# Context rows of a gated cross-attention kernel added by GpSimd besides vector, with the plan's places set anew

## What is computed

```python
txt_proj = jnp.einsum('btd,de->bte', textual_features, Ws)
feat_proj = jnp.einsum('bfd,de->bfe', features, W)
h = jnp.tanh(txt_proj[:, None, :, :] + feat_proj[:, :, None, :] + b[None, None, :, :][..., 0, :])
rho = jnp.einsum('bftd,d->bft', h, w[:, 0])
...
att = jax.nn.softmax(rho, axis=-1)
txt_h = jnp.einsum('bft,btd->bfd', att, textual_features)
w_s = jnp.tanh(jnp.einsum('bfd,od->bfo', txt_h, Wcw) + bcw)
b_s = jnp.tanh(jnp.einsum('bfd,od->bfo', txt_h, Wcb) + bcb)
return w_s * features + b_s
```

## Time and profile before

| | us |
|---|---|
| median of 3 runs | 1027.43 |
| lowest, highest | 1023.06, 1028.69 |
| span of the profiled execution | 1025.4 |
| TensorE products busy | 934.7 |
| ScalarE busy | 674.1 |
| GpSimd busy | 219.0 |

### The profile page before, as it was taken

The page is one execution under the profiler, slowest core; times in us unless marked ns, Lnnn a source line. Parts: engine busy times, 40 slices in busy tenths (PEclk is TensorE's granted clock), DMA queues, the critical chain, the costliest instruction groups (busy, mean ns, idle before and its releaser), DMA issues. The chain is left out here.

```text
span 1025.4 us, 22330 instructions
## 1 busy us (share of the span) xinstructions
PE 934.7 (91%) x8078; PEld 742.7 (72%) x8078; DVE 748.9 (73%) x1959; ACT 674.1 (66%) x983; POOL 219.0 (21%) x250
## 2 busy tenths in 40 slices
PE   8689999989988799999999999999999999985773
PEld 5557887779988787777777878888888887842331
DVE  3787988862222389978869869868876997795995
ACT  2122222201100069999999999989997998899992
POOL 1014543540112222312212211202211211220000
PEclk9579999999998899999999999999999999989886
DMA  7826677948996866756756667768777776410000
GB/s 247 338 62 236 244 267 283 351 174 279 331 338 227 272 232 226 236 165 219 237 175 228 211 202 253 267 219 277 266 253 231 268 260 220 149 32 12 2 22 21
DMA packets 137456, 218.68 MB, mean 213 GB/s; under 512 B 14113, under 2 KB 79138, under 8 KB 137346
## 3 DMA queue, kind: packets, MB, share of 16 engines
q1 hardware_dynamic: 119202, 156.55, 45.9%
q10 hardware_dynamic: 8592, 34.60, 8.7%
q0 software_dynamic: 9552, 26.10, 7.2%
HBM read 159.14 MB, written 58.06 MB: 212 GB/s over the span
## 5 line engine op out<-in xcount | busy, mean ns | idle before, releaser
L1287 PE MATMUL bank<-rowsT,expert_w 128*128 128x128 f32 x2656 | 328.3, 278 | 0.5 <-DVE rowsT L1053 0.5
L1287 PEld LDWEIGHTS bank<-rowsT,expert_w 128*128 128x128 f32 x2656 | 319.1, 194 | 9.5 <-issue 5.1
L748 ACT ACTIVATE tanhs<-shared_w,txtT 128x512 f32<-128x512 f32 x276 | 174.3, 718 | 24.5 <-issue 18.4
L748 ACT ACTIVATE arena<-shared_w,txtT 128x512 f32<-128x512 f32 x272 | 172.1, 720 | 0.0
L1458 PE MATMUL bank<-expert_w,act 128*128 128x256 f32 x664 | 162.4, 388 | 0.0
L1458 PEld LDWEIGHTS bank<-expert_w,act 128*128 128x128 f32 x664 | 121.7, 193 | 30.6 <-issue 17.3
L728 ACT ACTIVATE act<-bank 128x512 f32<-128x512 f32 x83 | 48.9, 589 | 114.2 <-PE bank L1287 114.2
L643 POOL DMA_DIRECT2D rows_by_expert<-rows_out x71 | 42.0, 592 | 371.4 <-DVE rows_out L1082 349.2
L654 POOL DMA_INDIRECT picked<-rows_by_expert,slot_of x64 | 75.9, 1186 | 157.6 <-issue 93.9
L1484 PE MATMUL bank<-arena,pick_w 128*32 128x256 f32 x1200 | 79.2, 389 | 3.2 <-ACT arena L737 2.3
L1484 PE MATMUL bank<-tanhs,pick_w 128*32 128x256 f32 x1112 | 74.4, 412 | 7.3 <-ACT tanhs L737 4.7
(11 more groups left out here) (257 smaller groups left out, 1392.1 us busy)
## 6 DMA issues: line engine op xcount, KB each, us to landing
expert_w<-in_WgT SPq DMA_DIRECT2D x71, 512.0 KB, 3.9
expert_w<-in_WuT SPq DMA_DIRECT2D x71, 512.0 KB, 5.2
expert_w<-in_WdT SPq DMA_DIRECT2D x71, 512.0 KB, 6.9
rows_by_expert<-tanhs ACTq DMA_DIRECT2D x8, 4096.0 KB, 14.3
rows_in<-rows_by_expert SPq DMA_DIRECT2D x71, 128.0 KB, 6.1
rows_by_expert<-rows_out POOLq DMA_DIRECT2D x71, 128.0 KB, 5.6
expert_w<-in_WgsT SPq DMA_DIRECT2D x12, 512.0 KB, 3.8
expert_w<-in_WusT SPq DMA_DIRECT2D x12, 512.0 KB, 4.6
```

The costliest lines, as they stand in the source:

```text
L748: got = e.activation(tiles[ec][:, S * j:S * (j + 1)], featT[ec], ACT.Tanh, bias=txtT[:, ec, t + j:t + j + 1])
L1287: got = e.matmul(bank[:, i * P:(i + 1) * P], w[:, at:at + P], t[:, c * P:(c + 1) * P], start=c == 0, stop=c == DC - 1)
```

## The change

Some pairs that were direct are now added by GpSimd: POOLS gives their number in each batch, counted over the pairs that vector does not add, and at most as many as there are of those. Its numbers sum to 77; in batch 7 there are 15 such pairs for 19, so 73 pairs result. A step `pooladd` does on GpSimd what `preadd` does on vector: two tensor_scalar of 128x512 for a channel half, after waiting for the feature copy and for the sum of the pair 8 before. ScalarE then waits for it and takes the pair in one activation. The next batch's feature copy on vector waits for the last of these adds, besides the last direct pair. PAIRS goes from 79 to 64 pairs, JOINS from 111 to 115. PLACES and LAGS get new numbers, which also puts the shared weights' load ahead of batch 0's x. The change is also described as letting tanh read the features in PSUM; there is no line for that in the diff, and featT stays in SBUF. The added pairs of batch 6 and 7 afterwards (v by vector, P by GpSimd, . direct, pair 0 first) are:

```diff
@@ -33,33 +33,39 @@
 
 ENGINES = ("sync", "gpsimd", "scalar", "vector", "tensor")
 
-PLACES = {"shared": -2.5, "zeroed": 62.5, "gap": 0, "opened": 25.5, "att_norm": 120, "att_norm_long": 30.5, "attend": 90,
-          "attend_long": 23.5, "moe_norm": 62, "moe_norm_long": 28, "route": 28, "route_long": 34, "late": -59, "gather": 4.5,
-          "norm": 2, "add": 7, "mix_in_end": -0.5, "join": 6.5, "sum": 5, "preadd": 4, "mix_out": 9.5, "mix_out_end": 49}
-
-
-PAIRS = {0: 18, 1: 9, 2: 12, 3: 0, 4: 0, 5: 0, 6: 13, 7: 27}
-JOINS = {0: 16, 1: 8, 2: 6, 3: 28, 4: 24, 5: 28, 6: 1, 7: 0}
+PLACES = {"shared": -2.5, "zeroed": 54, "gap": 0, "opened": 38, "att_norm": 120, "att_norm_long": 29.5, "attend": 90,
+          "attend_long": 23, "moe_norm": 62, "moe_norm_long": 28, "route": 28, "route_long": 33.5, "late": -58, "gather": 4.5,
+          "norm": 2, "add": 7, "mix_in_end": -0.5, "join": 7, "sum": 5, "preadd": 4, "pooladd": 4.5, "mix_out": 9.5,
+          "mix_out_end": 49}
+
+
+PAIRS = {0: 17, 1: 12, 2: 6, 3: 0, 4: 0, 5: 0, 6: 12, 7: 17}
+POOLS = {0: 5, 1: 10, 2: 5, 3: 8, 4: 1, 5: 16, 6: 13, 7: 19}
+JOINS = {0: 16, 1: 9, 2: 6, 3: 28, 4: 28, 5: 28, 6: 0, 7: 0}
 
 
 WARM = {"start": 14, "turn_rho": 2, "turn_q": 4, "linear": 0}
 
 
 LAGS = {
...
-    "gpsimd": {"narrow": 1.5, ("power", "att"): -3.5, ("power", "lin"): -2, "scatter": -0.5},
...
+    "sync": {"fetch": -17.5, "keep": 7.5, "linear": 1.5, "load_late": -2.5, "load_shared": -11.5, "load_side": -6, "load_x": 1.5,
+               "narrow": 0.5},
+    "gpsimd": {"gather": -1, "narrow": 0.5, "pooladd": -1.5, ("power", "att"): -3.5, ("power", "lin"): -2, ("power", "mix"): -2,
+               ("power", "moe"): 1, "scatter": -1},
...
@@ -177,6 +183,12 @@
 
         pairs, share = self.T // 2, int(PAIRS[b])
         return m * share // pairs != (m + 1) * share // pairs
+
+    def pooled(self, b, m):
+
+        rest = [k for k in range(self.T // 2) if not self.added(b, k)]
+        pairs, share = len(rest), min(int(POOLS[b]), len(rest))
+        return m in rest and rest.index(m) * share // pairs != (rest.index(m) + 1) * share // pairs
 
     def joined(self, b, m):
 
@@ -236,6 +248,10 @@
                     for ec in range(2):
                         early = max(at, at + 2 * m + ec - PLACES["preadd"])
                         place([[("preadd", b, ec, m)]], early, early)
+                if self.pooled(b, m):
+                    for ec in range(2):
+                        early = max(at, at + 2 * m + ec - PLACES["pooladd"])
+                        place([[("pooladd", b, ec, m)]], early, early)
                 if self.joined(b, m):
                     late = at + 2 * m + PLACES["join"]
                     place([[("join", b, m)]], late, late)
@@ -443,6 +459,7 @@
         s_shared_mm, s_x_shared = sem("shared_product"), sem("x_shared_added")
         s_added = sem("x_expert_added")
         s_wide_in, s_wide, s_sum = sem("wide_added"), sem("wide_tanh"), sem("rho_product")
+        s_pool_in = sem("wide_added_by_pool")
         s_joined, s_larger, s_swapped = sem("wide_joined"), sem("larger_ready"), sem("features_swapped")
         s_rho, s_rho_sub, s_rho_e = sem("rho_read"), sem("rho_less_max"), sem("rho_exp")
         s_ws, s_squash, s_affine, s_applied = sem("weighed"), sem("squashed"), sem("affine_ready"), sem("x_affine")
@@ -641,6 +658,17 @@
                     tile = e.value_load(tile_at[0:1, r:r + 1], min_val=0, max_val=ABSENT + 7)
                     e.wait_ge(s_row_bank, row_no["narrow", n] + 1)
                     e.dma_start(rows_dram[bass.ds(tile * P, P), :], rows_out[r % OUTS][:, :]).then_inc(s_stored[r % OUTS], 16)
+                elif name == "pooladd":
+                    b, ec, m = k
+                    q = pair_of(b, m)
+                    w = halves_of[q % PAIR][ec]
+                    bank, use, _ = misc["feature", b, ec]
+                    e.wait_ge(s_misc[bank], use)
+                    if q >= PAIR:
+                        e.wait_ge(s_sum, q - PAIR + 1)
+                    t = b * T + 2 * m
+                    e.tensor_scalar(w[:, 0:S], featT[ec], txtT[:, ec, t:t + 1], None, ALU.add)
+                    e.tensor_scalar(w[:, S:2 * S], featT[ec], txtT[:, ec, t + 1:t + 2], None, ALU.add).then_inc(s_pool_in, 1)
                 elif name == "gather":
                     b, j = k
                     u = 2 * ST * b + j
@@ -735,6 +763,9 @@
                     if plan.added(b, m):
                         e.wait_ge(s_wide_in, wide_in_no[b, DC - 1, m] + 1)
                         e.activation(wide_pair[q % PAIR], wide_pair[q % PAIR], ACT.Tanh).then_inc(s_wide, 1)
+                    elif plan.pooled(b, m):
+                        e.wait_ge(s_pool_in, pool_in_no[b, DC - 1, m] + 1)
+                        e.activation(wide_pair[q % PAIR], wide_pair[q % PAIR], ACT.Tanh).then_inc(s_wide, 1)
                     else:
                         if m == 0:
                             for ec in range(DC):
@@ -760,6 +791,8 @@
                     e.activation(weighed[:, 0, :], weighed[:, 0, :], ACT.Tanh, bias=scal[:, BCW:BCW + 1])
                     e.activation(weighed[:, 1, :], weighed[:, 1, :], ACT.Tanh, bias=scal[:, BCB:BCB + 1]).then_inc(s_squash, 1)
 
+        pool_in_no = {s[1:]: i for i, s in enumerate(s for s in plan.of["gpsimd"] if s[0] == "pooladd")}
+        assert list(pool_in_no) == sorted(pool_in_no, key=lambda k: (k[0], k[2], k[1]))
         wide_in_no = {s[1:]: i for i, s in enumerate(s for s in plan.of["vector"] if s[0] == "preadd")}
         joined_no = {s[1:]: i for i, s in enumerate(s for s in plan.of["vector"] if s[0] == "join")}
         assert list(wide_in_no) == sorted(wide_in_no, key=lambda k: (k[0], k[2], k[1])) and list(joined_no) == sorted(joined_no)
@@ -1106,7 +1139,10 @@
                 elif name == "feature":
                     b, ec = k
                     bank, done = product(("feature", b, ec))
-                    read = [m for m in range(T // 2) if b and not plan.added(b - 1, m)]
+                    read = [m for m in range(T // 2) if b and not plan.added(b - 1, m) and not plan.pooled(b - 1, m)]
+                    pool = [k for k in pool_in_no if k[0] < b]
+                    if pool:
+                        e.wait_ge(s_pool_in, pool_in_no[pool[-1]] + 1)
                     if read:
                         e.wait_ge(s_wide, pair_of(b - 1, read[-1]) + 1)
                     if wide_in_no and b and plan.added(b - 1, T // 2 - 1):
```

More of the change, by code:

```diff
@@ L45 @@
+PAIRS = {0: 17, 1: 12, 2: 6, 3: 0, 4: 0, 5: 0, 6: 12, 7: 17}
+POOLS = {0: 5, 1: 10, 2: 5, 3: 8, 4: 1, 5: 16, 6: 13, 7: 19}
+JOINS = {0: 16, 1: 9, 2: 6, 3: 28, 4: 28, 5: 28, 6: 0, 7: 0}
 WARM = {"start": 14, "turn_rho": 2, "turn_q": 4, "linear": 0}
 LAGS = {
-    "sync": {"fetch": -21, "load_side": -5.5, "narrow": 0.5},
-    "gpsimd": {"narrow": 1.5, ("power", "att"): -3.5, ("power", "lin"): -2, "scatter": -0.5},
-    "scalar": {"gate_act": 1, "soft_rho": -0.5, "softmax": -1, "spread": -2, "squash": 2, "tanh": 1, ("turn", "att"): -0.5,
-               "turn_e": -3.5, "zero": 8},
@@ L53 @@
-    "vector": {"add": 1.5, "add_bias": 4, "affine": 0.5, ("aggr", "att"): 1, ("aggr", "lin"): -0.5, ("aggr", "mix"): 1.5,
-               ("aggr", "moe"): -0.5, "apply": 2.5, "choice": -1, "convert": -16.5, "gate_act": 2.5, "join": -1, "larger": -9,
-               "linear": 3.5, "narrow": 1.5, ("newton", "att"): -2, ("newton", "lin"): -1.5, ("newton", "mix"): 0.5,
-               ("newton", "moe"): 1, "opened": 1.5, "pads": -1, "place": -0.5, ("power", "att"): -0.5, ("power", "lin"): 1,
-               ("power", "mix"): 0.5, ("power", "moe"): -1.5, "rho": -4, "side": -7, "sigmoid": -0.5, "soft_rho": -1, "softmax": 0.5,
-               ("stats", "att"): 2.5, ("stats", "mix"): 3.5, "step": -0.5, "stretch": 1, "sums": 1.5, "swap": -4, "text": -0.5,
-               "tiles": 2, ("turn", "mix"): -0.5, ("turn", "moe"): -4, "turn_q": 0.5, "turn_rho": -1, "turn_rows": 1, "weigh": -1,
-               "weigh_ws": -0.5},
@@ L61 @@
-    "tensor": {"count": 2, "feature": -0.5, "larger": -2, "logits": -2.5, "narrow": 0.5, "scores": -1.5, "spread": 3, "sum": -1,
-               "text": -1, ("turn", "att"): -1, "turn_e": -3.5, "turn_rho": -3, "up": -1, "weigh": -0.5},
+    "sync": {"fetch": -17.5, "keep": 7.5, "linear": 1.5, "load_late": -2.5, "load_shared": -11.5, "load_side": -6, "load_x": 1.5,
+               "narrow": 0.5},
+    "gpsimd": {"gather": -1, "narrow": 0.5, "pooladd": -1.5, ("power", "att"): -3.5, ("power", "lin"): -2, ("power", "mix"): -2,
+               ("power", "moe"): 1, "scatter": -1},
@@ new lines @@
+    "scalar": {"gate_act": 1, "soft_rho": -0.5, "softmax": -1.5, "spread": 3.5, "squash": 2, "tanh": 1, ("turn", "att"): -0.5,
+               ("turn", "moe"): -2, "turn_e": -2, "zero": -3.5},
+    "vector": {"add": 1, "add_bias": 4, "affine": -1, ("aggr", "att"): 0.5, ("aggr", "lin"): 0.5, ("aggr", "mix"): 1,
```

(11 more changed lines are left out.)

## The result

The changed kernel takes 1174.89 us (median of 4 runs, 1173.96 to 1177.77), the one before 1027.6 (median of 4; the table ahead has 3 of them): a ratio of 1.147 (95% interval 1.144 to 1.151), 147 us slower. The forecast was 1019 us with a range that ended at 1038. The profiled execution has a span of 1173.2.

What follows compares the result with a forecast made beforehand. Two bounds in series: TensorE to about 900 us, then ScalarE. From 1027.4 us, 8.4 off for ScalarE, 1.9 off for joins, 2 added for the feature chain: 1019 us; own range 1013 to 1024, 8-in-10 range 1011 to 1038.

Steps and rivals of the forecast that it cites:

- GpSimd's adds: the unknown cost: Price of one 128x512 add on GpSimd: taken as 0.8 us, bounds 0.47 to 0.86, so 3.2 us a pair.
- Costed at nothing, on that cover: GpSimd's adds stand 7 plan steps ahead of their tanh, 10 us in batch 5, 6.3 in batch 7: cost 0.
- GpSimd paces batch 7: Rival: adds of 0.86 us never overlap vector's pre-adds, so GpSimd sets batch 7's pace; 1028 us, chance 0.22.
- Head of line: Rival: a gather's wait in GpSimd's queue delays adds, 3 us a batch in four batches; 1031 us, chance 0.07.
- One port for two engines: Rival: GpSimd's adds and vector's operations shut each other out, mainly batches 5 and 7; 1037 us, chance 0.18.
- ScalarE, the term that pays: Behind the last gate activation, 13 direct pairs become pre-added, saving 0.65 us each: 8.4 us off the end.
- What is late next: Batch 7's feature chain (gather, norm, transposes, products) ties with ScalarE's end of batch 6: 2 us added, 0 to 4.
- no gain in the middle: Before about 895 us TensorE is the bound, so ScalarE's savings there buy nothing.
- the joins of batch 4: Four more joins in batch 4 save TensorE 0.48 us each: 1.9 us off.
- the places near 0: New places, including the shared weights' loads ahead of batch 0's x: -2 to +4 us together, taken as 0.
- the feature copy's new wait: Vector's feature copies wait for GpSimd's last add of the batch before: one new wait on the path.
- the marks set for "wrong": Signs against the forecast: longer pre-adds or joins, adds well above 0.9 us, tanhs waiting for GpSimd, TensorE waiting in batch 5.

Runs made afterwards that it cites:

- b5_8: The kernel before with GpSimd adds for 8 pairs of batch 5 alone, every fourth pair: 1035.17 us, ratio 1.009.
- two_inputs: The changed kernel with GpSimd's adds as tensor_tensor against the broadcast context column instead of tensor_scalar: 1200.21 us, ratio 1.172 to the kernel before.
- mixed6: The kernel before with four direct pairs of batch 6 added half by vector, half by GpSimd, and batch 7's feature products ahead of the sums: ratio 1.004.
- micro: The kernel before with GpSimd and vector instructions appended behind its last result, executed once: a 512-column add takes 1.55 us alone, 1.86 beside vector's pre-adds.
- cols64: The changed kernel with each GpSimd add cut to 64 of its 512 columns (sums partly wrong): 1020.54 us, ratio 0.995 to the kernel before.
- vec6: As mixed6, but vector adds both halves of the four pairs and GpSimd adds nothing: ratio 1.000 to the kernel before.
- late_only: The changed kernel with GpSimd adds in batches 6 and 7 alone, none in batches 0 to 5: ratio 1.078 to the kernel before.
- cols64_first: As cols64, with batch 7's feature products placed earlier on TensorE, ahead of the sums: ratio 0.997 to the kernel before.

## Why the prediction was wrong, by its own steps

**The step that failed: "GpSimd's adds: the unknown cost".** Its term was 0.8 us an add with an upper bound of 0.86; measured 1.55 alone and about 1.77 in the kernel. The bound was drawn through a memset of 4 columns and one select of 128 and carried to 512 at 1.5 ns a column, while the tensor_scalar takes 2.5. An instruction of another kind gave no upper bound, and nothing in the trace of before showed a tensor_scalar or anything of 512 columns that reads. The Trainium skill, GPSIMD Engine Reference, section Elementwise, which the prediction drew on, gives 769 ns for 512 elements of a tight loop and doesn't say that the loop is a tensor_scalar; this case measured 1.55 us for that instruction, and the measurement decides. That the two agreed (0.8 and 0.77) made the number look firmer than it was. The same text said that at 0.9 us an add no longer fits batch 7: the whole result hung on a limit 12% above the value taken. With 7.1 us for the pair, GpSimd's work in a stage adds up to the 130, 104 and 108 us of the section above. With 1.55 for the add alone, without any conflict, batch 5 would need 16 x 6.2 + 16.5 = 116 us. So of the 42 us lost there about 26 are the plain price and 14 the conflict, an estimate from these numbers.

**"Costed at nothing, on that cover".** The cover was counted in lead for one pair (10 us), not in GpSimd's total for a stage. A lead hides a latency once; 16 x 3.2 + 16.5 = 68 of 91 us held only at the assumed price.

**The rival "GpSimd paces batch 7"** was the right mechanism, in batches 5 and 6 too (and perhaps in batch 1, which no run tried alone), but priced with the same 0.86: 1028 us. **"Head of line"** is confirmed in kind; its size is two to three times the 3 us a batch that was put: 6.3 us for three badly placed pairs, 10.2 for the eight of b5_8. **"One port for two engines"** is confirmed in kind. It was to decide from 0.25 us of vector's time for each add. In batch 5 of the after, vector is busy 88.4 us for 75.2, 13.2 us over 64 adds or 0.21 us an add, and has 132.7 us for it: with tensor_scalar the conflict lengthens the adds but doesn't make vector the pace. In two_inputs it does. The prediction quoted from the Trainium skill, SBUF — State Buffer, section Who interferes with whom, that the later starter blocks fully. The join of two_inputs that started during an add and lasted 6.43 us agrees with it. The add of mixed6 doesn't: it started 0.04 us before vector's work, and it was the add that was long. Nor does micro, where 8 adds and 12 pre-adds that need 12.4 and 4.8 us alone were through in 13.8 together. The measurements decide.

**"ScalarE, the term that pays", 8.4 us.** Right, where GpSimd doesn't pace. With the adds cut to 64 columns ScalarE's busy time from the last gate activation to the last tanh falls from 107.6 to 99.5 us, 8.1 of 8.4. The stretch falls by 4.4, since 3.7 us come back as waits: 1.43 for a step of vector, 0.45 for a GpSimd pair, and 1.84 at batch 7's first pair (933.29, L768, waiting for GpSimd).

**"What is late next"** named the right chain and gave it 2 us; it takes 1.84 in cols64 and 1.81 in vec6. The size is in part luck. The prediction had the feature products 5 us sooner than before (929 for 934); in cols64 they start 39.5 us behind the last gate activation, before 39.1, so not sooner at all, and ScalarE comes late as well by its other waits. The expectation of vec6 erred in this chain too: it read vector's room as 33 of 45 us busy, but 9.95 of the idle 12 us is one wait at the end of the chain. Ahead of it vector is nearly full (17.3 of 18 us in vec6), so pre-adds put there delay batch 7's features.

**Right:** no gain in the middle, where TensorE is the bound (batch 5 of cols64 90.4 us for 90.3); the joins of batch 4 worth 1.5 us (91.9 to 90.4 in late_only and cols64; 1.9 forecast); the places near 0, from the side of the start too; the feature copy's new wait, which came true as 8.05 us but only because GpSimd paced; and that no line lets tanh read PSUM. Of the marks set for "wrong", three of four came: adds above 0.9 us, tanhs waiting for GpSimd in batches 5 and 7, TensorE waiting in batch 5; pre-adds rose from 0.48 to means of 0.60 to 0.69 and joins from 1.28 to 1.30 to 1.37, the fourth in part.

**Open:** what of the 27.8 us in batches 0 to 3 is head of line and what pace; and the 5 us that batch 0 takes longer in late_only and cols64 (2 in cols64_first), with little or nothing of GpSimd in it. No run tried these alone. No version here beats the kernel before; cols64, which is 0.5% below it, leaves part of the sums out.

## What to carry to other kernels

Before giving an idle engine streaming work, measure that very instruction at that very size, alone and beside its neighbour; a different opcode's time per column is no upper bound, and where the sum turns at 12% above an assumed price, the price is the whole prediction. Then add up the engine's total for each stage, not only the lead of one step; and place steps on an in-order queue clear of those that wait for transfers. Read slack on an in-order engine from where its idle time lies: a wait at the end of a chain is no room for work ahead of that chain.
